# Layer 0's probabilities turned by DMA with scores pair by pair; layer 1's last rounding step on GpSimd, a cross pair between two self pairs

## The reference

```python
# layer 0: rmsnorm of x and ctx, 16 heads of 64, keys and values of 4 heads shared by 4 query heads each
p = softmax(q @ k.T * 0.125); x = x + (p @ v) @ wo
# layer 1: self attention, cross attention, gated feed-forward; heads of 16, all operands rounded to 8 bits
def _fq(x, delta, zp, n_bits):
    xi = round(x / delta) + zp
    return (clip(xi, 0, 2 ** n_bits - 1) - zp) * delta
attn = softmax(_fq(q, dq, 128, 8) @ _fq(k, dk, 128, 8).T * SCALE)
out  = _fq(attn, dw, 0, 8) @ _fq(v, dv, 128, 8)
# layer 2: cross attention, 16 heads of 64 with own keys and values each, relu feed-forward
# layer 3: causal self attention and cross attention, heads of 16, relu feed-forward
```

## Time and profile before

| | |
|---|---|
| median of three runs | 4849.15 us |
| the profiled execution, its own time | 4847.86 us |
| its span, first to last instruction | 4846.1 us |
| TensorE busy | 4440.9 us (92%) |
| VectorE busy | 2955.7 us (61%) |
| ScalarE busy | 2974.7 us (61%) |
| GpSimd busy | 2282.1 us (47%) |
| mean granted TensorE clock | 0.955 |

### The profile page before, as it was taken

How to read it: one execution, slowest core, us unless ns; L and a number is a source line. 1 busy time by engine, 2 the same in 40 slices (tenths; PEclk the granted TensorE clock), 3 DMA queues, 4 the chain that set the end, 5 groups by cost and what they waited for, 6 DMA issues and landing times.

```text
span 4846.1 us, 84907 instructions
## 1 busy us (share of the span) xinstructions
PE 4440.9 (92%) x30496; PEld 3230.0 (67%) x30496; DVE 2955.7 (61%) x6426; ACT 2974.7 (61%) x9009; POOL 2282.1 (47%) x4132
## 2 busy tenths in 40 slices
PE   8999999967787878789999999999999999999998
PEld 5666666646565656566666666666667777778777
DVE  6566566566666666666555555555555666667665
ACT  4555555688888888885444454444445666666664
POOL 3333333465656565664444444444444444444443
PEclk9999999979888888889999999999999999999999
DMA  2000000032333232343433333333332100000000
GB/s 85 21 21 24 21 21 22 25 90 62 62 61 64 61 62 63 61 86 68 98 76 77 75 74 77 77 74 74 77 76 47 41 19 19 18 19 19 18 18 7
DMA packets 631891, 249.53 MB, mean 51 GB/s; under 512 B 596784, under 2 KB 613424, under 8 KB 630064
## 3 DMA queue, kind: packets, MB, share of 16 engines
q1 hardware_dynamic: 631472, 244.10, 23.0%
HBM read 82.53 MB, written 14.68 MB: 20 GB/s over the span
## 4 chain that ended last, share of the span: by engine, by line
PE 82%; ACT 8%; POOL 4%; DVE 3%; issue 2%; DMA 2%; SPq 0%; ACTq 0%; POOLq 0%; DVEq 0%
PE ring L1437 51%; PE score L1366 11%; PE ring L1380 7%; ACT e L1563 5%; PE ring L1418 3%; PE ring L1411 3%; PE ring L1426 2%; DMA probs<-halves 2%; POOL e L1961 1%; POOL e L1964 1%; PE ring L1377 1%; PE ring L1401 1%; ACT work L1624 1%; PE ring L1452 1%; DVE nmax L1698 1%
## 5 line engine op out<-in xcount | busy, mean ns | idle before, releaser
L1964 POOL TENSOR_SCALAR e<-e,rsum 112x375 f32<-112x375 f32 (+1 forms) x2048 | 1102.2, 556 | 1677.4 <-DVE rsum L1705 1642.5
L1698 DVE TENSOR_REDUCE nmax<-score 112x2 f32<-112x750 f32 (+1 forms) x1152 | 1066.4, 951 | 407.0 <-PE score L1366 406.4
L1563 ACT ACTIVATE e<-score,nmax 112x375 f32<-112x375 f32 (+1 forms) x2048 | 1038.6, 537 | 117.8 <-DVE nmax L1698 115.5
L1437 PE MATMUL ring<-h,weights 128*128 128x224 f32 x3840 | 872.1, 369 | 34.5 <-ACT work L1624 24.9
L1437 PEld LDWEIGHTS ring<-h,weights 128*128 128x128 f32 x3840 | 734.3, 197 | 145.1 <-issue 52.7
L1366 PE MATMUL score<-keys,q 64*112 64x375 f32 (+2 forms) x3584 | 607.3, 493 | 235.4 <-ACT e L1563 231.4
L1603 ACT COPY probs<-ring 125x336 f32<-125x336 f32 (+1 forms) x625 | 252.5, 452 | 746.2 <-PE ring L1380 635.4
L1366 PEld LDWEIGHTS score<-keys,q 64*112 64x112 f32 (+2 forms) x3584 | 232.7, 166 | 539.0 <-ACT e L1563 289.5
L1437 PE MATMUL ring<-weights,ctx 128*128 128x512 f32 (+4 forms) x1536 | 587.1, 515 | 0.0
L1437 PE MATMUL ring<-ctx,weights 128*128 128x375 f32 x1536 | 567.2, 491 | 1.0 <-DVE heads L1799 0.8
L1563 ACT ACTIVATE e<-score,nmaxc,quant 112x375 f32<-112x375 f32 (+1 forms) x1024 | 555.1, 554 | 10.7
(11 more groups left out here) (128 smaller groups left out, 5782.1 us busy)
## 6 DMA issues: line engine op xcount, KB each, us to landing
ctx<-ctx_t SPq DMA_DIRECT2D x128, 375.0 KB, 3.1
out_t<-x SPq DMA_DIRECT2D x64, 224.0 KB, 2.0
x<-out_t SPq DMA_DIRECT2D x48, 224.0 KB, 2.6
weights<-weights SPq DMA_DIRECT2D x7, 1024.0 KB, 5.9
probs<-halves SPq DMA_TRANSPOSE x320, 2.7
planes<-halves SPq DMA_TRANSPOSE x256, 3.4
x<-x_t SPq DMA_DIRECT2D x16, 224.0 KB, 2.5
weights<-weights SPq DMA_DIRECT2D x1, 3328.0 KB, 11.5
```

What stands on the lines that cost most here:

```text
L1437: ins = pe.matmul(out_, a, b_, start=n == 0, stop=n == len(parts) - 1)
L1563: ins = nc.scalar.activation(e_of(u)[:, n * width:(n + 1) * width], score_bank(u)[0:S, n * width:(n + 1) * width], ACT.Exp, bias=minus, sc ...
L1698: ins = dve.tensor_reduce(to, src, AX, ALU.max, negate=True)
L1964: ins = nc.gpsimd.tensor_scalar(mine, mine, rsum[0:S, slot(u), n:n + 1], 0.0, ALU.mult, ALU.add)
```

## The change

- Layer 0's cross attention goes the way of layer 2 (WORDS = (0, 2)): split, flip and merge take the place of turn and copy. It no longer scores in quads (QUADS = (2, 3)). The output projection of layer 0 is planned 1.0 later.
- All splits are on GpSimd, all merges on VectorE, in layers 0 and 2.
- Layer 1's clips are all on GpSimd, behind the clamps; ScalarE's and VectorE's clips are removed.
- Layer 1's eights share the three slots of `halves` with the splits, in one count, where they had four slots of their own.
- In layer 1 the order is cross, cross, self, cross, self, cross.
- Some of the planner's costs are changed. GpSimd makes one constant fewer and waits for VectorE's setup before its first step.

```diff
-STEPSLOTS = 4
-WORDS = (2,)
-SPLIT_BY = ("V", "G")
+WORDS = (0, 2)
+SPLIT_BY = ("G",)
+MERGE_BY = "V"
 SPLITS = 3
 PLANES = 2
-QUADS = (0, 2, 3)
+QUADS = (2, 3)
...
                     for n in range(4):
                         self.pair(o)
-                        if beside and n == 1:
+                        if beside and layer == 1:
+                            if n in (1, 2):
+                                self.pair(beside)
+                        elif beside and n == 1:
                             self.pair(beside)
                             self.pair(beside)
...
     def halves_before(self, p):
 
-        i = self.nth_halved[p]
-        found = [self.halved[i - SPLITS]] if i >= SPLITS else []
...
+        i = self.nth_turned[p]
+        return [self.turned[i - SPLITS]] if i >= SPLITS else []
...
-        self.row(e + 3.5, e + 4.6, [("o", layer, s, 0, m, "V") for m in range(KC)])
+        late = 1.0 if layer == 0 else 0
+        self.row(e + 3.5 + late, e + 4.6 + late, [("o", layer, s, 0, m, "V") for m in range(KC)])
...
-                self.add("split", p, by, 1.7, p.index + 1.4)
-                self.add("flip", p, "D", 4.2, p.index + 1.6)
-                self.add("merge", p, "VA", 1.45, p.index + 2.4)
+                self.add("split", p, by, 1.7 if by == "G" else 1.1, p.index + 1.4)
+                self.add("flip", p, "D", 3.5, p.index + 1.6)
+                self.add("merge", p, MERGE_BY, 0.9 if MERGE_BY == "V" else 1.2, p.index + 2.4)
...
-                self.add("clip", j, "VA", self.clip_cost(j), j.pos + 0.5)
+                self.add("clip", j, "G", self.clip_cost(j), j.pos + 0.4)
...
+        def pool_clip(wait, j):
+            wait.wait_ge(clamped, nth["clamp", j])
+            rows, width = quantised_shape(j)
+            r = rounded[0:rows, j.place % 4, 0:width]
+            if j.kind in ("q", "q2"):
...
+                for odd in range(2):
+                    ins = nc.gpsimd.tensor_scalar(to[:, j.m, odd, :], r, qmask[:, a + odd:a + odd + 1],
+                                                  qshift[:, a + odd:a + odd + 1], ALU.mult, ALU.add)
+            elif j.kind in ("k", "ck"):
...
+                ins = nc.gpsimd.tensor_scalar(to, r, 1.0, -ROUND, ALU.mult, ALU.add)
+            else:
+                values_ready(wait, j)
+                for dst, src in value_parts(j, rounded[:, j.place % 4, :]):
+                    ins = nc.gpsimd.tensor_scalar(dst, src, 1.0, -ROUND, ALU.mult, ALU.add)
+            ins.then_inc(clipped, 1)
...
+            wait.wait_ge(setup_done, 1)
```

More of the change, by code:

```diff
@@ L231, in place_attention @@
         self.nth_halved = {p: i for i, p in enumerate(self.halved)}
-        self.ones = [p for p in self.pairs if p.octet.layer == 1]
-        self.nth_of_one = {p: i for i, p in enumerate(self.ones)}
+        self.turned = [p for p in self.pairs if p.octet.layer == 1 or self.in_words(p.octet)]
+        self.nth_turned = {p: i for i, p in enumerate(self.turned)}
         for p in self.pairs:
@@ L518, in before @@
             yield "weigh", x
-            for p in self.steps_before(x):
+            for p in self.halves_before(x):
                 yield "flip", p
@@ L873, in arrange @@
                 self.nth[step.kind, step.x] = counts[e, step.kind]
-                if step.kind == "clip":
-                    step.x.clip_by, step.x.clip_nth = e, counts[e, "clip"]
                 if step.kind == "merge":
@@ L988, in four_layers @@
         clamped = sem("clamped")
-        clipped = {"V": sem("clipped_v"), "A": sem("clipped_a")}
-        minus_magic = sb("minus_magic", [P, 1])
+        clipped = sem("clipped")
         qshift = sb("qshift", [P, 4])
@@ L1116, in steps_of @@
             runs = 4 if is_own(p.octet) else CHUNKS
-            return steps[0:S, plan.nth_of_one[p] % STEPSLOTS, 0:2 * runs * P]
+            return halves[0:S, plan.nth_turned[p] % SPLITS, 0:2 * runs * P].bitcast(BF16)
         def halves_of(p):
-            return halves[0:S, plan.nth_halved[p] % SPLITS, :]
+            return halves[0:S, plan.nth_turned[p] % SPLITS, :]
         def planes_of(p):
@@ L1247, in clips @@
             def clips(self, jobs):
-                for by in "VA":
-                    self.wait_ge(clipped[by], max([j.clip_nth for j in jobs if j.clip_by == by], default=0))
+                self.wait_ge(clipped, max([nth["clip", j] for j in jobs], default=0))
             def products(self, jobs):
@@ L1327, in tensor_program @@
             wait.wait_ge(consts_loaded, 16)
-            wait.wait_ge(consts_made, 8)
+            wait.wait_ge(consts_made, 7)
             for kind, x_ in plan.order["T"]:
@@ L1537, in scalar_program @@
                     nc.scalar.copy(to, src).then_inc(merged["A"], 1)
-                elif kind == "clip":
-                    scalar_clip(wait, x_)
                 else:
@@ L1568, in scalar_exp @@
             ins.then_inc(expd, 1)
[L1570 to L1594, removed]
         def scalar_save(act, wait, j, logs):
@@ L1737, in vector_program @@
                     wait.wait_ge(weighed, nth["weigh", p])
-                    for before in plan.steps_before(p):
+                    for before in plan.halves_before(p):
                         flip_done(wait, before)
@@ L1746, in vector_program @@
                     dve.tensor_scalar(to, src, ROUND + 255.0, ROUND, ALU.min, ALU.subtract).then_inc(stepped, 1)
-                elif kind == "clip":
-                    vector_clip(dve, wait, x_)
                 else:
                     vector_save(dve, wait, x_)
[L1752 to L1775, removed]
         def vector_save(dve, wait, j):
@@ L1895, in vector_setup @@
             dve.sem_inc(setup_done, 1)
+        def pool_clip(wait, j):
[3 more added lines that the diff above has]
+            if j.kind in ("q", "q2"):
+                attn = "cross" if j.kind == "q2" else "self"
+                a = 2 if j.kind == "q2" else 0
+                scores_done(wait, plan.query_users(1, attn, j.s))
+                to = masked_queries(1, attn, j.s)
+                for odd in range(2):
+                    ins = nc.gpsimd.tensor_scalar(to[:, j.m, odd, :], r, qmask[:, a + odd:a + odd + 1],
+                                                  qshift[:, a + odd:a + odd + 1], ALU.mult, ALU.add)
+            elif j.kind in ("k", "ck"):
+                if j.kind == "k":
+                    scores_done(wait, plan.own_keys_users(1, j.s))
+                    to = own_keys(1, j.s)[:, j.m, :]
+                else:
+                    scores_done(wait, plan.keys_users(plan.keys_user(1, j.b)))
+                    to = cross_keys(1, j.b)[:, j.m, :]
+                ins = nc.gpsimd.tensor_scalar(to, r, 1.0, -ROUND, ALU.mult, ALU.add)
+            else:
+                values_ready(wait, j)
+                for dst, src in value_parts(j, rounded[:, j.place % 4, :]):
+                    ins = nc.gpsimd.tensor_scalar(dst, src, 1.0, -ROUND, ALU.mult, ALU.add)
+            ins.then_inc(clipped, 1)
         def pool_program(pool):
@@ L1903, in pool_program @@
             nc.gpsimd.memset(magic[:, :], ROUND).then_inc(consts_made, 1)
-            nc.gpsimd.memset(minus_magic[:, :], -ROUND).then_inc(consts_made, 1)
             nc.gpsimd.memset(halves[:, :, :], 0).then_inc(consts_made, 1)
@@ L1936, in pool_program @@
                     nc.gpsimd.memset(values[:, at, 0:words], 0.0).then_inc(zeroed, 1)
+                    continue
+                if kind == "clip":
+                    pool_clip(wait, x_)
                     continue
@@ L2000, in sync_program @@
                     wait.done([plan.pv_of[o] for o in plan.probs_before(p.octet)])
-                    sp.dma_start(flipped(p), steps_of(p), transpose=True).then_inc(turned[n % FLIPS], 16)
+                    sp.dma_start(flipped(p).bitcast(U16), steps_of(p).bitcast(U16), transpose=True).then_inc(turned[n % FLIPS], 16)
                 elif kind == "store":
```

4 lines of the change are left out of this document (removed).

## The result

The changed kernel takes 4924.44 us (median of four runs, 4921.57 to 4929.64) against 4849.31 for the kernel before on the same chip: ratio 1.0155, 95% interval 1.0138 to 1.0173, slower. The forecast was 4890 in a range of 4700 to 5030, slower with a chance of 0.63.

A forecast was written before the change was run, and what follows sets the result against it. TensorE was taken to bound layers 0 and 2, with no engine full in layer 1. From 4847.9 us, +68 in layer 0, -27 in layer 1 and nothing in layers 2 and 3 gave 4890 us, range 4700 to 5030.

The forecast's parts named there:

- GpSimd becomes the bound of layer 0: Layer 0: GpSimd's 47.9 us a stream rises to 59.4 if all 16 merges collide, and sets the pace.
- Waits of 2.6 us: Layer 0: 2.6 us a stream added for waits between four loaded engines, giving 62.0 us.
- TensorE at 47.8 us: Layer 0: TensorE falls from 57.4 to 47.8 us a stream, less 11.2 of transposes, plus 1.6 for scores.
- The term for the scores pair by pair: Layer 0, TensorE: leaving quads costs 0.1 us a pair, 1.6 a stream, bounds 0 and 4.4.
- Layer 1 at -27 us: Layer 1: relief of ScalarE, order, GpSimd's added work and the lost slot sum to -1.7 us a stream.
- if that keeps the clock up: Layer 1: a cross pair between self pairs holds TensorE's clock over eight products, saving 1.7 us a stream.
- The slot: Layer 1: one slot of four for turned pairs is lost, costing 1.0 us a stream in waits before flips.
- The clips: Layer 1: clips moved to GpSimd save 1.7 us a stream through ScalarE and cost 0.7 through GpSimd.
- Rival A: Layer 0: merges find GpSimd idle, 49.9 us a stream, gaining 126 us, so 4696 us; chance 0.20.
- Rival B: Layer 1: all of ScalarE's relief counts, -109 us instead of -27, so 4808 us; chance 0.12.
- Rival C: Layer 1: becomes bound by GpSimd, 86.7 us a stream, +111 us, so 5028 us; chance 0.18.
- Rival D: Layers 0 and 1 cancel, leaving 4849 us; chance 0.05.

The follow-up runs named there:

- e1: The changed kernel with all merges on ScalarE in place of VectorE; 4845.96 us, ratio 0.9991 to the kernel before.
- e12: The kernel before with layer 0's scores pair by pair in place of quads, nothing else; 4918.37 us, ratio 1.0143.
- e6: The kernel before with layer 1's order cross, cross, self, cross, self, cross, nothing else; 4872.59 us, ratio 1.0048.
- e5: The kernel before with three slots in place of four for layer 1's turned pairs, nothing else; 4873.42 us, ratio 1.0049.
- e7: The kernel before with all clips of layer 1 on GpSimd, nothing else; 4840.04 us, ratio 0.9979.
- e4: The kernel before with layer 0's part and three slots, merges on ScalarE, splits on VectorE and GpSimd in turn; 4898.44 us, ratio 1.0096.
- e10: e9 with layer 0's scores in quads again; 4897.42 us.
- e2: The kernel before with layer 0's part of the change alone, merges on VectorE, three slots in layer 1; 4916.50 us, ratio 1.0135.
- e8: The changed kernel with four slots for layer 1's turned pairs from its first cross pair on; 4926.51 us, ratio 1.0159.
- e9: The kernel before with layer 0's part, merges on ScalarE, layer 1's clips on GpSimd, old order, four slots; 4807.49 us, ratio 0.9913.
- e11: e9 with merges on whichever of ScalarE and VectorE the planner finds free; 4826.58 us.

## Why the prediction was right, and where not

**GpSimd becomes the bound of layer 0: right.** Its load was put at 47.9 us a stream and 59.4 with the merges; 474.22 / 8 = 59.3 was measured, and 48.1 in e1, where no merge is on VectorE. The merge was put at 0.72 us of GpSimd's time. Per pair, two splits at 1044 - 827 and two weighs at 749 - 588 ns over their medians make 0.76; over the means of e1 they make 0.66. Merges are held up in their turn, 1.12 us for 0.84. The rule that the prediction weighed (the Trainium skill, SBUF — State Buffer, Who interferes with whom) is that whoever issues first holds the shared port pair for the whole instruction and the other fully blocks. The trace agrees that each holds up the other; the full 0.84 for each merge would be the 61.3 of the prediction, and 59.3 was measured.

**Waits of 2.6 us: too many.** The pace is 60.2, not 62.0; GpSimd is occupied 98%. The middle streams lost 27 us in all. The fill (10.7 us) and the last stream (19.5), more than half of the loss, were not in the sum. That layer 0 lost 57 us where 68 were forecast is luck: two errors offset each other.

**TensorE at 47.8 us: too low.** The term for the scores pair by pair, 0.1 a pair or 1.6 us a stream, was about right for the scores themselves (0.085 a pair in e12). The step that failed was to leave all the rest of TensorE's stream as it was. In e12, nine streams, TensorE is busy 3.3 us a stream more than before and idle 1.6 more, so the edit costs 4.3 a stream over the kernel, at the upper bound of 4.4. In e1, where no merge holds GpSimd up, TensorE is busy 51.0 us of 54.5. In the change it is busy 416.77 / 8 = 52.1 of 60.2, which GpSimd covers. Where the 3 us between 47.8 and 51.0 come from is open; the granted clock is 0.96 in e1 for 1.00 before.

**Layer 1 at -27 us: wrong, +23 measured.** The step that failed is "if that keeps the clock up", -1.7 us a stream for the order: the order alone costs 23 us, the eight products take 3.36 us as before, and the mean clock is 0.83 for 0.85 (e6). The slot, +1.0 a stream or 16 us, costs 24 alone (e5). The clips, -1.0 a stream or 16 us, gain 9 alone (e7). And adding them was wrong too: the prediction took each by its share in the chain, and the parts that cost 24 and 23 us cost 23 together. Why they do not add is open.

**The time, 4924 for 4890.** Of the 34 us between them layer 0 is 11 less than forecast, layer 1 50 more, layers 2 and 3 together 6 less. "Slower" came from layer 0, where the mechanism was right; with -27 us in layer 1 the time would still have been some 25 us over the one before. Two of the signs named in advance did not come: TensorE is busy 86% in layer 0 (75 to 85%), and GpSimd 70% in layer 1 (above 75%).

**Layer 2 unchanged: right,** 723.00 of 723 us again. **Rival A** (merges find GpSimd idle) fell: GpSimd's loss is that of all 16 merges. With the merges elsewhere it would have been right in sign for layer 0: e1 is that kernel, at 54.5 us a stream where A had 49.9. **Rival B** fell by sign. **Rival C** got the sign of layer 1, not the mechanism: GpSimd is busy 458.20 of 656 us there and no bound. **Rival D** fell: the layers do not cancel, both lose.

Open: why splits on both engines (e4) make layer 0 slower; what the fill and the last stream of layer 0 would take with another plan; whether the loop of two planes costs anything once the merges are on ScalarE, as a third plane was not tried.

## What to carry to other kernels

When work goes from the bounding engine to an idle one, add up the receiver's new load together with what locks it: here 38 us a stream of moved and blocked time (21.6 to 59.3) turned the emptiest engine (37% busy) into the bound at 98%, and moving one copy of 0.84 us to an engine that takes 1.46 us for it was worth 78 us. Price an edit in a stage without a full engine by a run of each part and of all together; shares of the chain did not price it here, and two parts that cost 24 and 23 us alone cost 23 together. Scores in quads were worth 69 us while TensorE was the bound (e12) and cost 90 where it was not (e10).

## What the runs showed of the hardware that was not expected

Layer 1's middle streams came to few lengths. Six different layer 1s were measured. The mean of eight streams, store to store, is 81.9 to 82.0 us in four of them: three slots (e2 to e5), the new order (e6), the new order with clips on GpSimd (e8), and this with three slots (the change, e1). It is 78.5 with the clips alone (e7, e9 to e11) and 80.0 in the kernel before and e12, which alternate between about 79.3 and 81. The granted clock is 0.88 to 0.89 at the short length. It does not explain the long one: it is 0.83 to 0.85 there, and 0.85 in the kernel before. Why four programs share a length is not shown.

A merge on VectorE is paid on both engines: GpSimd loses 0.66 to 0.76 us and VectorE 0.28 in the mean, for a copy that takes 0.84 at the shortest.
